# First task's operand rows of an attention layer made on the chip by 0/1 products instead of a trip through DRAM

## What is computed

```python
h = _layernorm(x) * (1 + ca) + sa
Q = (h @ W_dq @ W_uq).reshape(B, S, 16, 8)
K = (h @ W_dkv @ W_uk).reshape(B, S, 16, 8)
V = (h @ W_dkv @ W_uv).reshape(B, S, 16, 8)
scores = einsum('bqhd,bkhd->bhqk', Q, K) / sqrt(8)      # causal
x = x + ga * (softmax(scores) @ V) @ W_o
h = _layernorm(x) * (1 + cb) + sb
x = x + gb * ffn(h)                                     # 8 experts, top 2, and a shared one
```

## Time and profile before

| | |
|---|---|
| median of 3 runs | 458.31 us (457.81 to 459.12) |
| the profiled execution | 456.95 us |
| its span in the trace | 455.2 us |
| PE busy | 418.0 us, 92% |
| DVE busy | 319.0 us, 70% |
| ACT busy | 268.6 us, 59% |
| POOL busy | 149.7 us, 33% |
| granted TensorE clock | 0.965 (mean) |

### The profile page before, as it was taken

The page is one execution under the profiler, slowest core; times in us unless marked ns, Lnnn a source line. Parts: engine busy times, 40 slices in busy tenths (PEclk is TensorE's granted clock), DMA queues, the critical chain, the costliest instruction groups (busy, mean ns, idle before and its releaser), DMA issues.

```text
span 455.2 us, 9450 instructions
## 1 busy us (share of the span) xinstructions
PE 418.0 (92%) x2963; PEld 242.9 (53%) x2963; DVE 319.0 (70%) x1185; ACT 268.6 (59%) x611; POOL 149.7 (33%) x244
## 2 busy tenths in 40 slices
PE   6989899999999999989799998999889689999985
PEld 3444334534435444544234434337658469999945
DVE  5679889788879888896956884256676345555635
ACT  3558365576767676755543676867356154445661
POOL 2248100260100201064832335040663733333420
PEclk9999999999999999999977999999979979999998
DMA  5244150330402103004000002940111222210135
GB/s 146 65 142 140 49 163 1 108 139 1 108 1 62 47 0 106 3 0 102 6 19 13 20 26 65 322 101 11 41 46 54 76 65 78 65 38 27 37 122 174
DMA packets 28796, 31.78 MB, mean 70 GB/s; under 512 B 4827, under 2 KB 23363, under 8 KB 28243
## 3 DMA queue, kind: packets, MB, share of 16 engines
q1 hardware_dynamic: 25959, 25.82, 19.7%
q0 software_dynamic: 2272, 4.67, 3.0%
q10 hardware_dynamic: 516, 0.69, 0.5%
HBM read 21.04 MB, written 9.85 MB: 68 GB/s over the span
## 4 chain that ended last, share of the span: by engine, by line
PE 68%; DVE 14%; issue 6%; DMA 4%; ACT 3%; POOL 1%; another core or an unknown queue 1%; SPq 1%; ACTq 0%; DVEq 0%; POOLq 0%
PE oacc L1724 15%; PE sc L1700 11%; PE mx L1669 10%; PE sc L1857 7%; PE oacc L1872 6%; DVE mxp L1285 4%; DVE masked L1281 3%; PE sc L1705 2%; PE mx L1824 2%; PE mx L1813 2%; PE mx L1733 2%; ACT osb L949 1%; ACT pr L1010 1%; DMA S<-negT 1%; DMA S<-first_q_parts 1%
## 5 line engine op out<-in xcount | busy, mean ns | idle before, releaser
L940 ACT ACTIVATE pr<-sc 128x512 f32<-128x512 f32 (+1 forms) x295 | 155.7, 579 | 90.4 <-PE sc L1705 46.5
L1281 DVE CUSTOM_DVE_ANT_0 masked<-mx,later 128x128 f32<-128x128 f32 (+3 forms) x256 | 111.3, 485 | 18.1 <-PE mx L1669 17.4
L1669 PE MATMUL mx<-S 72*128 72x512 bf16 (+3 forms) x384 | 111.5, 331 | 7.8 <-DVE mxp L1281 4.1
L1700 PE MATMUL sc<-S 75*128 75x512 bf16 (+3 forms) x371 | 109.6, 332 | 0.7 <-DMA S<-negT 0.7
L1285 DVE TENSOR_REDUCE mxp<-mx 128x1 f32<-128x512 f32 x128 | 82.2, 684 | 22.2 <-PE mx L1669 21.8
L1724 PE MATMUL oacc<-pr,vb 128*32 128x512 f32 (+3 forms) x768 | 77.2, 511 | 0.0
L1010 ACT ACTIVATE pr<-sc,bcur 128x128 f32<-128x128 f32 x156 | 44.4, 368 | 30.7 <-PE sc L1857 19.5
L1700 PEld LDWEIGHTS sc<-S 75*128 75x128 bf16 x371 | 34.8, 98 | 48.2 <-issue 23.8
L1669 PEld LDWEIGHTS mx<-S 72*128 72x128 bf16 x384 | 34.2, 98 | 48.8 <-DVE mxp L1281 23.9
L782 POOL DMA_INDIRECT token_results<-S,xrow x39 | 38.5, 986 | 62.4 <-DVE S L1422 60.5
L1872 PEld LDWEIGHTS oacc<-vb,pr 128*128 128x128 f32 x312 | 40.3, 198 | 12.7 <-ACT pr L1010 6.4
(11 more groups left out here) (294 smaller groups left out, 508.0 us busy)
## 6 DMA issues: line engine op xcount, KB each, us to landing
S<-k_parts SPq DMA_DIRECT2D x21, 192.0 KB
S<-q_parts SPq DMA_DIRECT2D x42, 96.0 KB
xrow<-slot_rows SPq DMA_DIRECT2D x39, 64.5 KB, 1.8
S<-in_we SPq DMA_DIRECT2D x1, 2048.0 KB, 9.7
S<-in_we SPq DMA_DIRECT2D x4, 512.0 KB, 10.2
parts<-token_results SPq DMA_DIRECT2D x4, 512.0 KB, 5.1
x_sb<-in_x SPq DMA_DIRECT2D x4, 256.0 KB, 3.4
out_y<-attn SPq DMA_DIRECT2D x4, 256.0 KB, 2.3
```

The costliest lines, as they stand in the source:

```text
L940: act.activation(pr[:, group % NBUF, h:h + n, at:at + w], src, ACT.Exp, scale=float(DK) ** -0.5).then_inc(s["exp_done"], 1)
L1281: ins = dve.tensor_tensor_reduce(masked[:, d % 2, w * m:w * m + w], unit[a][:, w * m:w * m + w], later[:, HALF - w:HALF], 1.0, LOWEST, ALU ...
L1669: ins = pe.matmul(dst[:, w * m:w * m + w], S3[0:CROSS, r3, 1, q:q + P], S3[0:CROSS, r3, 0, kk:kk + w], start=(m == 0), stop=True, skip_gro ...
L1700: ins = pe.matmul(dst[:, w * m:w * m + w], S3[0:CROSS + 3, r3, 0, kk:kk + P], S3[0:CROSS + 3, r3, 1, q:q + w], start=(m == 0), stop=True, ...
```

## The change

The first half (tokens 0 to 511) of task 0's rows no longer goes through DRAM.

- GpSimd builds six 0/1 matrices (`picks`, bf16, one for K and one for Q per part, with 72 columns for each of 4 heads) in a free part of `pr`, before the first split: one MEMSET and six copies out of the identity.
- TensorE multiplies `parts` by them: `pick_rows(n, ...)` with n = 0 (K, heads 0 and 1), 1 (Q, heads 0 and 1), 2 (K, heads 2 and 3), 3 (Q, heads 2 and 3), six products of 128x512 each, accumulating the three parts. Two heads fill two PSUM banks.
- ScalarE copies each pair of banks into `S3`: `rows_out(n)`, 72x1024, four of them. TensorE's first max unit waits for the fourth (`rows_out` at 4).
- The second half keeps its trip through DRAM, in another order: Q pieces ahead of K pieces, and the load of Q ahead of those of K. The diagonal units of the second half wait for K (`first_k`), the others only for Q (`first_q`).
- V of the first batch row (`("val", 0, 0)`, `("val", 1, 0)`) moves from the start into the max units, behind (0, 3) and (0, 7). `warm(3)` behind the second `x_turn` and `warm(18)` go; 4 unneeded products stand before the first max unit. On ScalarE the copies of the transposed third and fourth groups (`h_out(2)`, `h_out(3)`) now follow the loading of the table for Exp. On VectorE `residue(3)` goes ahead of `rstd` of the last group.

```diff
-BETWEEN = {(0, 6): [("xturn", 2, 0)], (0, 9): [("xturn", 3, 0)], (0, 11): [("proj", 4, 0)], ...
+BETWEEN = {(0, 3): [("val", 0, 0)], (0, 7): [("val", 1, 0)], (0, 6): [("xturn", 2, 0)], (0, 9): [("xturn", 3, 0)], (0, 11): [("proj", 4, 0)], ...
-        QK = [(b, kq, half) for b in range(B) for half in range(2) for kq in range(2)]
-        qk_bank = [bank[2], oacc[:, 0, :], oacc[:, 1, :]]
+        QK = [(0, 0, 0), (0, 1, 0), (0, 1, 1), (0, 0, 1)] + [(1, kq, half) for half in range(2) for kq in range(2)]
+        qk_bank = [bank[2], oacc[:, 0, :], mx[:, 2, :], bank[2]]
+        picks = pr[:, 0, :, :].rearrange("p h n -> p (h n)").bitcast(BF16)[:, 0:2 * 3 * HQ * CROSS].rearrange(
+            "p (s a h r) -> p s a h r", s=2, a=3, h=HQ)
+        rows_bank = [mx[:, 0:2, :], oacc[:, 0:2, :], sc[:, 0:2, :], mx[:, 0:2, :]]
...
-            def store_first(half):
+            def store_first():
...
-                    for kq in range(2):
+                    for kq in (1, 0):
...
+            def load_first():
+
+                sp.wait_ge(s["q_out"], 48)
+                sp.dma_start(S3[0:CROSS, 1, 1, QW:2 * QW],
+                             q0.rearrange("a d h n -> (a d) (h n)").unsqueeze(1).broadcast_to([3 * DK, 3, QW])
+                             ).then_inc(s["first_q"], 16)
+                sp.wait_ge(s["k_out"], 48)
+                load_k(0, slice(HALF, S), s["first_k"])
...
-            for c in range(2):
-                store_first(c)
-                sp.wait_ge(s["k_out"], 48 * c + 48)
-                load_k(0, slice(HALF * c, HALF * c + HALF), s[f"first_in{c}"])
-                if c:
-                    load_first_q(sp, c)
+            store_first()
+            load_first()
             store_parts(0)
             neg_rows(0, 0)
...
+            chained(pool.memset(picks[:, :, :, :, :].rearrange("p s a h r -> p (s a h r)"), 0.0))
+            unit_of = identb[0:HQ * DK, 0:HQ * DK].rearrange("p (d h) -> p h d", h=HQ)
+            for part in range(3):
+                pool.tensor_copy(picks[0:HQ * DK, 0, part, :, :].rearrange("p h (r d a) -> p h r d a", r=3, a=3)[:, :, :, :, part],
+                                 unit_of.unsqueeze(2).broadcast_to([HQ * DK, HQ, 3, DK])).then_inc(s["sel_ready"], 1)
+                pool.tensor_copy(picks[0:HQ * DK, 1, part, :, 3 * DK * part:3 * DK * part + 3 * DK].rearrange("p h (d r) -> p h d r", r=3),
+                                 unit_of.unsqueeze(3).broadcast_to([HQ * DK, HQ, DK, 3])).then_inc(s["sel_ready"], 1)
...
+            def rows_out(n):
+
+                kq, h = n % 2, n // 2 * 2
+                act.wait_ge(s["rows_ready"], n + 1)
+                dst = (S3[0:CROSS, 1, 0, :].rearrange("r (h n) -> r h n", h=HQ)[:, h:h + 2, 0:HALF],
+                       S3[0:CROSS, 1, 1, 0:QW].rearrange("r (h n) -> r h n", h=HQ)[:, h:h + 2, :])[kq]
+                act.activation(dst, rows_bank[n][0:CROSS], ACT.Copy).then_inc(s["rows_out"], 1)
...
+            def pick_rows(n, parts_of):
+
+                kq, h = n % 2, n // 2 * 2
+                for part in parts_of:
+                    for m in range(2):
+                        ins = pe.matmul(rows_bank[n][0:CROSS, m, :], picks[:, kq, part, h + m, :],
+                                        parts[:, kq, part, 0:HALF], start=(part == 0), stop=(part == 2))
+                return ins
...
+                if t == 0 and k == 0:
+                    pe.wait_ge(s["rows_out"], 4)
+                if t == 0 and k == LAST_MAX[0] + 1:
+                    pe.wait_ge(s["first_q"], 16)
+                if t == 0 and c and diagonal:
+                    pe.wait_ge(s["first_k"], 48)
```

82 lines of the change are left out of this document (42 added, 40 removed).

## The result

The change makes the kernel faster, by more than was forecast: 454.75 us (median of 6, 454.37 to 457.3) against 457.59 (6 runs, 456.71 to 459.12) of the kernel before beside it, a ratio of 0.9943 with its interval [0.9915, 0.997]. Forecast were 458.1, and 456.9 to 459.7 as the range. The 458.31 that the forecast was added to was the median of three runs; with three more it is 457.59.

The account below looks back on a forecast made before the run. VectorE's unbroken run from k = 20, reached through the first 60 us, was taken as the bound. Terms -0.95, +0.85, -0.39 gave -0.5; the unmoved score unit returned 0.3, leaving -0.2: 458.1 us, range 456.9 to 459.7.

Parts of the forecast that it names:

- the issue of the nine stores: SyncE, after the K loads: nine stores take 6.25 us as before, until 35.45, so the negative maxima go at 35.5.
- TensorE's wait ahead of the second V unit: First block: TensorE there at 28.0, ScalarE's copy of the first V unit done only at 28.85; k = 8 on VectorE at 30.2.
- no wait for Q or K: Second block: Q lands by 29.95, winning another 0.39 us at k = 12; K, there before 33, is needed at 34.
- the -0.5 on VectorE: VectorE at the `negT` copy, 34.75: first max unit -0.95, V inside the first block +0.85, no Q wait -0.39.
- The first score unit: TensorE: goes at 37.9 as before, held by SyncE's transfer at 35.5; k = 20 on VectorE at 38.6, 0.2 us won.
- The spare 0.56 us is eaten: SyncE: its slack before the `negT` transfer vanishes, since the second half's traffic starts later; transfer at 35.5 as before.
- gives 0.3 of it back: Sum: the unmoved score unit takes 0.3 us of VectorE's -0.5, leaving -0.2.
- A microsecond won or lost in the first 60 us is carried to the end as it is: Whole kernel: TensorE is busy 49.4 of 50 us from 60 us on, so early gains carry unchanged.
- The first: VectorE without a gap from 23.64: k = 20 at 36.7, 2.2 us earlier, 456.1 us; chance 0.10.
- The second: ScalarE's table switch costs another 1.28 us, delaying the second V unit and k = 8: 459.1 us; chance 0.06.
- The third: Second half late: copies at 1.19 us, last `mid` 0.75 later, landing 0.8 later; +1.55, 459.7 us; chance 0.13.
- The fourth: TensorE falls to 1.2 GHz during the picks, adding 2.6 + 1.8 + 2.6 us: 465 us; chance 0.03.

Follow-up runs that it names:

- b_same: The kernel before, unedited, measured and profiled again: 456.66 us against 456.12, ratio 1.0009.
- a_same: The changed kernel, unedited, measured and profiled again: 455.54 us against 456.12 for the kernel before, ratio 0.9973.
- a_late2: The changed kernel with two unneeded 512-column products behind the first score unit: 455.49 us against 456.12 for the kernel before, ratio 0.9979.
- a_third: The changed kernel once more, without a further edit, on another chip: 438.82 us against 441.26 for the kernel before, ratio 0.994.
- a_best: Changed kernel, first V unit copied earlier, `negT` transfer ahead of the last four stores, fewer unneeded products: 438.19 us against 441.26 for the kernel before.
- a_bestkeep: The edits of a_best plus eleven unneeded products in the wait near 224 us: 436.11 us against 441.26 for the kernel before, ratio 0.9889.
- a_both: Changed kernel, first V unit copied after the fifth normalisation, `negT` transfer ahead of the last two stores: 439.17 us against 441.54 for the kernel before.
- b_qfirst: The kernel before with only the second half's order changed, Q ahead of K, rows still through DRAM: 440.05 us against 441.54, ratio 0.9947.

## Why the prediction was wrong in size, and what in it was right

The direction was right. One term of the sum, the issue of the nine stores, was mis-sized, and one statement on what lies behind the first 60 us was false. A part of the distance is neither: the forecast was added to 458.31, and the kernel before measured 457.59 beside the change, which is 0.7 us of the 3.35 between 458.1 and 454.75.

**Right, by its steps.** The matrices were built by 7.6 us. The first max unit was forecast at 23.15 and went at 23.19; a 72x1024 copy took 1.02 and 1.01 us against 1.0, and the last `mid` was done at 23.56 against 23.6. In the first block VectorE came to k = 8 at 30.17 against 30.2 and had been idle for 1.24 us against about 1.2; TensorE's wait ahead of the second V unit, 0.39 us, is there. In the second block there was no wait for Q or K: VectorE began it at 32.23 against 32.25, and started the `negT` copy at 34.62 against 34.75. So the -0.5 on VectorE is what the profile shows: 0.63 at that copy.

**The term that was mis-sized.** "The first score unit": "then the nine stores, which took 34.94 - 28.69 = 6.25 us: 35.45 ... The spare 0.56 us is eaten". The row was right for that execution of the kernel before and wrong for the changed one. The stores took 5.77 us in its first profile and 5.60 and 5.46 in the next two, which puts them out just about when VectorE's copy is done. So the score unit did move, by 0.45, and k = 20 came at 38.17, not 38.6, with no gap in front of it on VectorE. Of the sum's "gives 0.3 of it back" nothing is left: 0.66 us were won at k = 20, not 0.2. Had the transfer gone at 35.5, the rest of the step would have held: in b_same, where it went late, k = 20 started 3.07 us behind it, which gives 38.6. From the common date, the gain at k = 20 is 0.64 us for after against before and 1.0 for a_same against b_same, whose stores took 7.17 us, which the single profile of before could not show. A duration that differs by 0.9 us between two executions of one kernel was carried over as if it were fixed, and the range had no bound for it below. Why the stores are shorter in the changed kernel stays open.

**The part that the sum denied.** "A microsecond won or lost in the first 60 us is carried to the end as it is, and nothing behind them is touched." The first half is right: the twelve profiles above carry k = 20 to 180 us within 0.3. What it leaves out is the clock: it falls at several places (behind the wait near 224 in every profile without products in it; 81 to 89, 201 to 208, 241 to 250 in some) for 3 to 10 us, and those that could be priced cost 1.6 us (201 to 208, 242 to 250) and 2.7 (81 to 89). Which falls come differs between executions. The change itself is worth some 1.1 us (0.97 and 1.14 on two chips at the same clock). In the two first profiles 1.5 of the 2.0 us came by the fall at 242. For the medians' 2.84 us the rest is not located: the mean clocks of the six runs of the kernel before in that comparison are not on record, so that it came by the clock is likely and not shown. That the change makes falls rarer is neither shown nor excluded: on one chip the whole difference was 0.9 us, on another 2.4, and the dear fall at 81 to 89 stands in three (a_same, a_late2, a_third) of ten profiles with rows picked on chip, a_best and a_bestkeep left aside, and in none of the six with rows through DRAM.

**The rivals.** The first, the whole early start carried, did not happen. It named two conditions, V not waiting and `negT` free, and a_both shows that they are not enough: there was a third, TensorE's unneeded products in the first block. With that one moved too, a_best has k = 20 1.7 to 1.9 us before the two profiles of the kernel before, of the 2.2 that the rival gave. The second fell: behind the table load of 1.28 us the next instruction starts 0.01 later, as before. So the drain of about 1.38 us that the Trainium skill adds to a switch ("ScalarE: Activation LUTs", What ACT_TABLE_LOAD costs) is not to be seen in either kernel. The third did not happen: the copies took 1.02 us, and the stores were out half a microsecond before the forecast date and not after it. The fourth did not happen where it was looked for: the twelve picks from 14.79 on ran at full speed and the third projection began at 17.39, against 17.4. The clock fell elsewhere.

**What the change is made of.** Its name is the picking on chip, and it brings the first max unit 0.9 to 1.3 us forward; V and the unneeded products inside the first block use that up. What gives its 1.1 us is the order of the second half: Q projected, split and loaded ahead of K. b_qfirst has it with a few lines changed and gives 1.30 and 1.09 us in its two runs. Picking added nothing to that order and cost 1.2 us of k = 20 with K's loads first.

## What to carry to other kernels

Where a change does several things, time each of them alone: here the main part gave nothing until three limits behind it were moved, and a reordering beside it gave all. Before a difference of half a per cent between two profiles is explained, follow a date that recurs (here each task's `negT` transfer) through both and see where the lead is won: a jump far behind the changed code is the clock's, and the mean granted clock of each run says how much to take off. A queue that has under a microsecond to spare needs bounds for its issue times from more than one execution.

## What the runs showed of the hardware

- **The clock falls in a kernel that keeps TensorE busy for 91% of the span.** It is granted 0.50 several times for 3 to 10 us. Ahead of the fall at 226 in a_both it had been busy for 0.25 of 2 us, in a wait of 2.7; products in that wait kept 1.00 in both kernels that had them. In a_same, ahead of the fall at 81, it was never idle for long, but had just issued eight products of two columns:

```profile
79.19 1.02 PE L1676 MATMUL mx<-cs,wmod_sb 128*128 128x2 f32 x8
```

  They alone do not bring it: after has the same eight at 79.78 and before at 80.26, and neither falls there. What does was not found.
- **The same queue issues the same stores at different speeds.** Six transfers of `q_parts` took SyncE 2.87 to 4.76 us to issue, the three of `k_parts` ahead of them 2.35 to 3.25 (a_best).
- **The first rise of the clock has no fixed date.** Full speed is there at 11.08 in b_qfirst and not yet at 11.77 in before; the second `hT` copy came at 14.29 to 15.65 us, and all dates behind it moved along. The profile's granted clock reads 1.00 from the start of the span, so this first stretch at half speed is seen in the durations of the products alone.
- **Chips differ by 3%**: the kernel before took 456.12 and 455.95 us on two, 441.54 and 441.26 on two others, and the change was worth about as much on both sorts (0.97 and 1.14 us at the same clock). The clock takes part: all ten profiles of the slower sort have falls at 331 to 341 and at 362 to 376, and none of the eight of the other has one there. By the slopes above the difference of the mean clocks, 0.970 against 0.983, is worth some 3 of the 15 us.
